# A four-layer graph network on one core: bias and edge-mean products taken out of the layer products, and edge lists of 214 instead of 216 rows per partition

## The reference, cut to what matters

```python
h = relu(layernorm(x))
# layer 0: attention over all edges in both directions, 4 heads, then two dense products
out = segment_sum(gr[dst] * alpha, src)
x = x + gelu(concat([out, h]) @ W1.T + b1) @ W2.T + b2
# layer 1: two rounds; nbr_r, the mean of the edge attributes at dst, is the same in both
nbr_r = segment_sum(edge_attr, dst) * inv_deg
nbr_x = segment_sum(h[src], dst) * inv_deg
h = relu(concat([h, nbr_x, nbr_r]) @ W + b)
# layer 2: one round of the same kind, without the edge attributes
y = concat([h[tgt], h[src] - h[tgt]]) @ W + b, then the mean over the edges of a node
# layer 3: attention with 8 heads, layer norm, a feed-forward product with biases, layer norm
```

## Time and profile before

| what | value |
|---|---|
| median of 3 runs | 5928.51 us (5918.02 to 5931.22) |
| profiled execution, own time | 5926.62 us |
| its span | 5923.7 us |
| busy share DVE, POOL, PE, ACT | 68%, 60%, 45%, 21% |
| mean granted TensorE clock | 0.607 of full speed |

### The profile page before, as it was taken

One profiled execution on the slowest core, in us unless ns is written; L12 is line 12 of the kernel. 1 busy time (PEld: TensorE's weight loads), 2 busy tenths in 40 slices (PEclk: granted clock), 3 DMA queues, 4 the chain that ended last, 5 costly groups with the idle time before them and its releaser, 6 DMA issues.

```text
span 5923.7 us, 53534 instructions
## 1 busy us (share of the span) xinstructions
PE 2662.1 (45%) x13332; PEld 1808.8 (31%) x13333; DVE 4000.1 (68%) x6981; ACT 1264.8 (21%) x4424; POOL 3582.9 (60%) x3760
## 2 busy tenths in 40 slices
PE   1795101011211323333333542776762777777646
PEld 1570101001211323323322442554641323323215
DVE  9778888888875777877877882223232676767655
ACT  0000000000000111111111110000001777777731
POOL 2777777777777777777777743000005777777730
PEclk6555555555555555555555555767765888888876
DMA  6222121212222333333333320635431223323230
GB/s 234 58 58 50 49 55 49 76 41 51 51 65 55 84 78 85 77 80 83 78 81 80 86 70 22 215 105 172 135 99 23 73 82 82 84 80 89 73 101 6
DMA packets 391629, 476.62 MB, mean 80 GB/s; under 512 B 215693, under 2 KB 251599, under 8 KB 384256
## 3 DMA queue, kind: packets, MB, share of 16 engines
q1 hardware_dynamic: 135840, 279.78, 14.4%
q0 software_dynamic: 114832, 133.36, 11.0%
q10 hardware_dynamic: 140752, 61.28, 3.7%
HBM read 294.88 MB, written 179.24 MB: 80 GB/s over the span
## 4 chain that ended last, share of the span: by engine, by line
POOL 50%; issue 20%; DVE 13%; PE 11%; DMA 5%; ACT 0%; POOLq 0%; DVEq 0%; SPq 0%; ACTq 0%
POOL arena L779 35%; POOL rec_dram L736 11%; PE acc L2039 4%; DMA oh<-mt_dram 2%; DVE OHX L1473 2%; PE acc L1854 2%; PE acc L1856 1%; PE acc L2023 1%; POOL own_dram L756 1%; DMA V<-in_edge_attr_dram 1%; DMA rec_dram<-V,rowst 1%; PE acc L1990 1%; DVE oh L1483 1%; DVE arena L1495 1%; DVE V L1515 1%
## 5 line engine op out<-in xcount | busy, mean ns | idle before, releaser
L779 POOL DMA_INDIRECT arena<-tab_dram,jst x2592 | 2519.3, 972 | 778.1 <-issue 775.0
L736 POOL DMA_INDIRECT rec_dram<-V,rowst x784 | 837.5, 1068 | 231.6 <-issue 224.0
L729 POOL TENSOR_TENSOR pdum<-pdum 128x1 f32<-128x1 f32 x197 | 53.1, 270 | 1122.5 <-DVE arena L1681 869.3
L1982 PE MATMUL pw<-OHX 128*128 128x128 bf16 x1632 | 209.3, 308 | 789.3 <-DVE OHX L1473 788.7
L1990 PE MATMUL acc<-arena,oh 128*128 128x64 f32 x1952 | 423.1, 417 | 252.0 <-DVE oh L1483 252.0
L1990 PEld LDWEIGHTS acc<-arena,oh 128*128 128x128 f32 x1952 | 413.3, 327 | 266.3 <-issue 266.3
L946 ACT ACTIVATE arena<-arena,ew 128x64 f32<-128x64 f32 x1728 | 417.8, 333 | 33.4 <-PE acc L2063 33.4
L2063 PE MATMUL acc<-OHX,ident 128*128 128x512 f32 x432 | 253.8, 753 | 370.6 <-ACT OHX L946 370.6
L946 ACT ACTIVATE OHX<-arena,ew 128x64 f32<-128x64 f32 x1728 | 417.8, 333 | 2.5
L1982 PEld LDWEIGHTS pw<-OHX 128*128 128x128 bf16 x1632 | 155.8, 140 | 840.5 <-DVE OHX L1473 840.5
L1495 DVE TENSOR_TENSOR arena<-arena,pt 128x1024 f32<-128x1024 f32 x108 | 131.8, 1221 | 383.3 <-DMA arena<-tab_dram,jst 381.2
(11 more groups left out here) (535 smaller groups left out, 6281.4 us busy)
## 6 DMA issues: line engine op xcount, KB each, us to landing
oh<-mt_dram SPq DMA_DIRECT2D x90, 512.0 KB, 3.6
arena<-tab_dram,jst POOLq DMA_INDIRECT x2592, 2.5
arena<-rec_dram SPq DMA_DIRECT2D x122, 288.0 KB, 3.6
mt_dram<-oh ACTq DMA_DIRECT2D x272, 128.0 KB, 1.8
oh<-mt_dram SPq DMA_DIRECT2D x75, 416.0 KB, 3.9
oh<-mt_dram SPq DMA_DIRECT2D x75, 384.0 KB, 3.9
rows_dram<-V SPq DMA_DIRECT2D x27, 1056.0 KB, 4.0
rows_dram<-arena SPq DMA_DIRECT2D x27, 1056.0 KB, 4.3
```

Source lines behind the costliest of these rows:

```text
L736: gp.indirect_dma_start(rec[:, :], bass.IndirectOffsetOnAxis(ap=rowst[:, q, k:k + 1], axis=0), recst[:, q, k, :], None).then_inc(S[f"scat{ ...
L779: gp.indirect_dma_start(hd.G[:, a.r, j, :], None, table[:, :], row_of(jst[:, a.r, j:j + 1])).then_inc(S[f"{x}g{a.r}"], 16)
L1982: last = nc.tensor.matmul(unit_bank(c.slot)[:, k // 2 * P:(k // 2 + 1) * P], mones[c.slot][:, 0, k, :], mones[c.slot][:, 1, k, :], start=k ...
```

## The change

1. RU = 214 rows per partition are used; the layout in DRAM keeps its 216. In the last block of each list the last two rows are empty, so 24 gathers are issued there instead of 32 (blocks 26 and 53 of layer 0, block 26 of layer 3), and DVE waits for as many (`gathered`). POOL's loop over the blocks of layer 0 is cut in two, with blocks 24 to 27 written out between.
2. The transposes of nbr_r and its products with both rounds' W1b are made once, while POOL runs the 50 gathers at the end of layer 0. DVE adds the bias to each and keeps the results in NBW (SBUF). The transposes use tile pw. In the same wait DVE adds the bias of layer 0's second product to X.
3. No product has a bias matmul any more. DVE adds NBW or the broadcast bias to the product after it (rounds 0 to 2); in the last feed-forward product DVE adds the bias to Hn while PE works.
4. The copy of Hn into CAT moves from the end of each round to its start.
5. `bias` is a tile of 128 partitions, filled by broadcasting DMAs at the start. `row_index` and the list stage have one small DVE instruction more for each call.

```diff
--- before.py
+++ after.py
 RP, RB, RK = 216, 8, 4
+RU = 214
 RH = RB // 2
 TB = RB * RK
 NBL = RP // RB
 NB0, NB3 = 2 * NBL, NBL
-ROWS = P * RP
...
+        NBW = [OHXf[:, k * NC * D:(k + 1) * NC * D].rearrange("p (c d) -> p c d", d=D) for k in (2, 3)]
...
+        def short(a):
+
+            return isinstance(a.g, int) and a.g % NBL == NBL - 1
+
+        def gathered(a):
+
+            done = (a.turn + 1) * TB
+            if isinstance(a.g, int):
+                done -= sum(last <= a.g and last % 4 == a.r for last in range(NBL - 1, NB0, NBL)) * (RP - RU) * RK
+            return done * 16
...
-                sp.dma_start(bias[:, k, :], t[name].unsqueeze(0)).then_inc(S["wts"], 16)
+                sp.dma_start(bias[:, k, :], t[name].unsqueeze(0).to_broadcast([P, D])).then_inc(S["wts"], 16)
...
-                sp.dma_start(LB[:, l, :], lin[l][0:P * RP * RK].rearrange("(p x) -> p x", p=P)).then_inc(S["lbi"], 16)
+                sp.dma_start(LB[:, l, 0:RU * RK], lin[l][0:P * RU * RK].rearrange("(p x) -> p x", p=P)).then_inc(S["lbi"], 16)
...
                     hold(S[f"{x}j{a.r}"], (a.turn + 1) * 16, held[0] + a.g)
-                    for j in range(TB):
+                    for j in range(TB - (RP - RU) * RK if short(a) else TB):
                         gp.indirect_dma_start(hd.G[:, a.r, j, :], None, table[:, :], row_of(jst[:, a.r, j:j + 1])).then_inc(S[f"{x}g{a.r}"], 16)
                 if hd is heads0:
                     quads(gp, n, rows, 0, KEYS_AT // 4)
                     held[0] += KEYS_AT
                     gather_keys()
                     held[0] -= KEYS_AT
-                    quads(gp, n, rows, KEYS_AT // 4)
+                    quads(gp, n, rows, KEYS_AT // 4, NBL // 4)
+                    for t in range(4):
+                        rows(Group(NBL // 4, t))
+                    quads(gp, n, rows, NBL // 4 + 1)
                 else:
                     quads(gp, n, rows)
                 held[0] += n
...
-            exponentials("a", [CX0[1], CX0[2], FC0, FX0])
+            exponentials("a", [CX0[1], CX0[2], FC0])
+            transposed(D, NRT, pw)
+            exponentials("a", [FX0], 3)
             transposed(2 * D)
             ff_up(0, ACT.Gelu, D, b1c0)
             sqrt_()
             transposed(2 * D)
-            transposed(D, NRT)
             transposed(2 * D)
             sqrt_()
...
-                link(V.tensor_scalar(spare, nid, each, unused3, ALU.mult, ALU.add))
-                elsewhere(val[:, 0:NC], spare[:, 0:NC])
-                link(V.tensor_copy(dst[:, 2, :], spare[:, 0:NC]))
-                link(V.tensor_scalar(rowi, val, 1.0 / RP, None, ALU.mult))
...
+                link(V.scalar_tensor_tensor(rest, quo, float(RP - RU), val, ALU.mult, ALU.add))
+                link(V.tensor_scalar(spare, nid, each, unused3, ALU.mult, ALU.add))
+                elsewhere(rest[:, 0:NC], spare[:, 0:NC])
+                link(V.tensor_copy(dst[:, 2, :], spare[:, 0:NC]))
+                link(V.scalar_tensor_tensor(val, quo, float(2 * RP - RU), val, ALU.mult, ALU.add))
...
+                link(V.memset(lb[:, RU * RK:RP * RK], float(KEYEND)))
...
-                v.wait_ge(S[f"{x}g{a.r}"], (a.turn + 1) * 16 * TB)
+                v.wait_ge(S[f"{x}g{a.r}"], gathered(a))
...
+            def bias_of(k):
+
+                return bias[:, k, :].unsqueeze(1).to_broadcast([P, NC, D])
+            v.wait_ge(S["lin"], 3)
+            V.tensor_tensor(NBW[0], acc_n, bias_of(1), ALU.add).then_inc(S["act"], 1)
+            v.wait_ge(S["act"], 3)
+            link(V.tensor_tensor(X[:], X[:], bias_of(0), ALU.add))
+            v.wait_ge(S["lin"], 4)
+            link(V.tensor_tensor(NBW[1], acc_n, bias_of(2), ALU.add))
             v.wait_ge(S["aeg"], 2 * NC * 16)
             EM = E0[:, :, :, w0:]
...
+                link(V.tensor_copy(CAT[:, :, 0:D], Hn[:]))
...
-                link(V.tensor_copy(CAT[:, :, 0:D], Hn[:]))
                 link(V.tensor_reduce(XC, SUM3.rearrange("p (c k d) -> p c d k", k=3, d=D), AX, ALU.add))
                 link(V.tensor_tensor(CAT[:, :, D:2 * D], XC, deg_b, ALU.mult))
                 if r == 2:
                     link(V.tensor_tensor(CAT[:, :, D:2 * D], CAT[:, :, D:2 * D], Hn[:], ALU.subtract))
                 V.memset(vdum[:, 0:1], 0.0).then_inc(S["ev"], 1)
-                v.wait_ge(S["lin"], 4 + r)
+                v.wait_ge(S["lin"], 6 + r)
+                link(V.tensor_tensor(XC, acc_n, NBW[r] if r < 2 else bias_of(3), ALU.add))
                 if r == 0:
-                    link(V.tensor_scalar(Hn[:], acc_n, 0.0, None, ALU.max))
+                    link(V.tensor_scalar(Hn[:], XC, 0.0, None, ALU.max))
                     split_rows()
                     continue
                 if r == 1:
-                    link(V.tensor_scalar(XC, acc_n, 0.0, None, ALU.max))
+                    link(V.tensor_scalar(XC, XC, 0.0, None, ALU.max))
                 else:
-                    link(V.tensor_tensor(XC, acc_n, hasin[:].unsqueeze(2).to_broadcast([P, NC, D]), ALU.mult))
+                    link(V.tensor_tensor(XC, XC, hasin[:].unsqueeze(2).to_broadcast([P, NC, D]), ALU.mult))
                 link(V.tensor_tensor(X[:], X[:], XC, ALU.add))
...
-            v.wait_ge(S["lin"], 8)
-            link(V.tensor_tensor(Hn[:], Hn[:], acc_n, ALU.add))
+            link(V.tensor_tensor(XC, Hn[:], bias_of(4), ALU.add))
+            v.wait_ge(S["lin"], 10)
+            link(V.tensor_tensor(Hn[:], XC, acc_n, ALU.add))
...
-            def product(parts, width, bk=None):
+            def product(parts, width):
 
                 pe.wait_ge(S["tc"], ntp[0])
                 for c in range(NC):
                     o = acc[:, c * width:(c + 1) * width]
                     for n, (TL, K, R) in enumerate(parts):
-                        last = nc.tensor.matmul(o, TL[0:K, c * P:(c + 1) * P], R, start=n == 0, stop=n == len(parts) - 1 and bk is None)
-                    if bk is not None:
-                        last = nc.tensor.matmul(o, ones[0:1, :], bias[:, bk, :], start=False, stop=True)
+                        last = nc.tensor.matmul(o, TL[0:K, c * P:(c + 1) * P], R, start=n == 0, stop=n == len(parts) - 1)
                 last.then_inc(S["lin"], 1)
 
             def hidden(W, K, n0):
...
+            transposes(nbr_r[:], D, pw)
+            for k in range(2):
+                if k:
+                    pe.wait_ge(S["act"], 3)
+                product([(NRT, D, W1b[:, k, :])], D)
             pe.wait_ge(S["ev"], 3)
             transposes(CAT, 2 * D)
             hidden(WT[:, 2, :], 2 * D, 0)
-            product([(T2, D, WT[0:D, 3, :])], D, 0)
+            product([(T2, D, WT[0:D, 3, :])], D)
 
...
-                if r == 0:
-                    transposes(nbr_r[:], D)
-                if r < 2:
-                    product([(T, 2 * D, W1a[:, r, :]), (NRT, D, W1b[:, r, :])], D, 1 + r)
-                else:
-                    product([(T, 2 * D, WT[:, 4, :])], D, 3)
+                product([(T, 2 * D, W1a[:, r, :] if r < 2 else WT[:, 4, :])], D)
...
-            product([(T2, 2 * D, F2[:])], D, 4)
+            product([(T2, 2 * D, F2[:])], D)
```

More of the change, by code:

```diff
@@ L54 @@
 NB0, NB3 = 2 * NBL, NBL
-ROWS = P * RP
+ROWS = P * RU
 MW = 2 * TB + 3 * RB
@@ L307, in build @@
         attb = sb("attb", [P, D])
-        bias = sb("bias", [1, 5, D])
+        bias = sb("bias", [P, 5, D])
         lnb = sb("lnb", [P, 5, D])
@@ L693, in _ @@
                 sp.wait_ge(S[f"dwr{q}"], 16 * NB3)
[L694 removed]
+            sp.dma_start(TL3, rows3[0:P * RP, :].rearrange("(p f) w -> p f w", p=P)[:, RU - 1, :]).then_inc(S["dtl"], 16)
             sp.wait_ge(S["xp"], 1)
@@ L833, in _, with transposed @@
             ntc, nln = [0], [0]
-            def transposed(K, dst=None):
+            def transposed(K, dst=None, frm=pt):
                 for b in range(-(-NC // 4)):
@@ L839, in transposed @@
                     bank = (ntc[0] % 2) * 512
-                    A.copy((T if dst is None else dst)[0:K, b * 512:b * 512 + m], pt[0:K, bank:bank + m]).then_inc(S["tc"], 1)
+                    A.copy((T if dst is None else dst)[0:K, b * 512:b * 512 + m], frm[0:K, bank:bank + m]).then_inc(S["tc"], 1)
                     ntc[0] += 1
@@ L883, in _, with exponentials @@
                 act.wait_ge(S[f"scat{q}"], SG * 16 * GT)
-            def exponentials(x, bufs):
+            def exponentials(x, bufs, done=0):
                 for k, buf in enumerate(bufs):
-                    act.wait_ge(S[x + "cx"], k + 1)
+                    act.wait_ge(S[x + "cx"], done + k + 1)
                     A.activation(buf, buf, ACT.Exp).then_inc(S[x + "cb"], 1)
@@ L1150, in row_index @@
             def row_index(dst, val, unused0, unused3, each):
-                link(V.tensor_scalar(spare, nid, each, unused3, ALU.mult, ALU.add))
-                elsewhere(val[:, 0:NC], spare[:, 0:NC])
-                link(V.tensor_copy(dst[:, 2, :], spare[:, 0:NC]))
```

(27 more changed lines are left out.)

3 lines of the change are left out of this document (1 added, 2 removed).

## The result

The changed kernel takes 5765.2 us (median of 4 runs, 5761.9 to 5767.3), the kernel before 5926.8 us beside it: a ratio of 0.9729 [0.9712, 0.9745]. The forecast was 5774 us, between 5757 and 5795 us. The profiled execution took 5767.3 us with a span of 5765.6 us, 158.1 us less span than before. Beside the first eight experiments the kernel before itself took 7911 us (chip 11) and 7916 us (chip 0), so that from those runs only short stretches of the trace can be used; beside the last four it took 5926.0 us (chip 2) and 5927.4 us (again a chip with the number 0).

A forecast was written before the change was run, and what follows sets the result against it. POOL's gathers pace the attention; in rounds and feed-forward parts DVE waits for PE's products. Products -134.3, X add +1.0, fewer gathers -9.9 and -9.9: -153.1 us from 5926.6, said as 5774 us, range 5757 to 5795.

The forecast's parts named there:

- What stays of the waits: DVE's five product waits keep 13.7 us (layer 0), 6.2 us in each round and 16.1 us (last).
- The products at 9.8, 9.8, 9.8, 9.8 and 10.9 us: Five products without bias matmuls take 50.1 us together instead of 184.4; 134.3 us saved, bounds 106.9 to 152.9.
- alternation: In products, taking turns between 128- or 64-row stationary tiles and the one-row tile costs extra: 0.31 us per instruction.
- rival B: The shorter products run at the fast clock from end to end: 18.6 us more saved, 5755 us; chance 0.07.
- The moved work at 0: Transposes, two products and adds, some 33 us, hide in layer 0's wait for 50 gathers, done over 30 us early.
- The X add at +1.0 us (0 to 1.8): DVE's add of the bias to X, both inputs in SBUF, holds POOL's gathers at layer 0's end: +1.0 us.
- Biases on DVE, copies moved, net 0: In the rounds three adds of about 1.85 us come, three copies of 1.82 us become hidden; +5.5 us without cover.
- Block 26 of layer 0, -9.9: Eight fewer gathers put POOL 9.9 us ahead, and all of it arrives at block 48: -9.9 us.
- block 53, 0: Layer 0's last block: DVE comes without a wait, so eight fewer gathers are worth 0, at most 9.9 us.
- Block 26 of layer 3, -9.9: Eight fewer gathers ahead of a DVE that waits 10.20 us in the last block: -9.9 us.
- Rival D: New lists make each of 2568 gathers dearer; 0.060 us each eats the gain, 0.07 gives 5953 us; chance 0.02.

The follow-up runs named there:

- bias_matmul_b: Changed kernel with one-row bias matmuls back behind each of the 25 matmuls of the three round products and the last product: 5856.3 us, ratio 0.9875.
- copy_at_end: Changed kernel with the copy of Hn into CAT back behind the neighbour sums of each round: 5767.5 us, ratio 0.9732.
- products_only_b: Changed kernel with lists of 216 rows per partition and all 2592 gathers again, run on another chip: 5780.5 us, ratio 0.9757.
- block26_full_b: Changed kernel with 32 gathers again in block 26 of layer 0 only: 5774.5 us, ratio 0.9743.
- extra_128: Changed kernel with one more 128-row accumulating matmul behind each of 25 in four products: waits 60.7 us (rounds), 32.2 us (last product).
- products_only: Changed kernel with lists of 216 rows per partition and all 2592 gathers again: 7753 us beside 7911 us, ratio 0.982.

## Why the prediction was right, step by step

**What stays of the waits**: right. The waits are 20.6 us for layer 0, 38.5 for the rounds and 27.3 for the last product with the covered add (forecast 23.5, 3 x 16 and 27), 86.4 us together. Without their products, 38.9 us, they keep 47.5 us, where the forecast kept 48.4 (13.7 + 3 x 6.2 + 16.1).

**The products at 9.8, 9.8, 9.8, 9.8 and 10.9 us**: the mechanism, alternation, was right and is shown; the size was 11.2 us off (50.1 forecast, 38.9 measured). The term that was mis-sized is the clock. I took it that four products begin fast and slow down on the way, as the one at 33.25 us does. In rounds 1 and 2 the granted clock was 1.00 until the product ended; in layer 0 and round 0 it fell on the way (0.54 from 3640.00 to 3644.30 us in layer 0's). The windows of the changed kernel over the product of round 1 and the second half of round 0's (engines' busy us and instructions, PEclk, DMA share, GB/s):

```profile
4083.00:4089.00 6.00, 5.79 (x50) 5.66 (x50) 0.08 (x1) 0.04 (x1) 0.00 (x0) 1.00 0.00 0
3871.00:3875.50 4.50, 4.48 (x21) 4.29 (x21) 0.00 (x0) 0.00 (x0) 0.00 (x0) 0.50 0.00 0
```

So rival B was right for two of the five products, and 146.4 us lies between the forecast 134.3 and its bound of 152.9.
The rule of the Trainium skill behind B (TensorE: Matmul & The Clock Gate, "What's actually happening": the throttled clock is the default and activity releases it) fits rounds 1 and 2. It does not fit round 0, nor this window of bias_matmul_b, in which PE is never idle and stays at 0.50:

```profile
4364.00:4390.00 26.00, 26.00 (x86) 21.02 (x85) 0.00 (x0) 0.00 (x0) 0.00 (x0) 0.50 0.00 1
```

**The moved work at 0**: right. The second moved product ended at 3563.4, the last add at 3565.4, and the gathers landed at 3611.0; 45.7 us were left, more than the 30 forecast; the first product, for one, took 6.87 us where 10.9 was taken for it.

**The X add at +1.0 us (0 to 1.8)**: it holds POOL, by less. DVE's line 1630 and the gather beside it:

```profile
3552.49 1.86 DVE L1630 TENSOR_TENSOR X<-X,bias 128x1600 f32<-128x1600 f32 x1
```

```profile
3552.50 0.95 POOL L825 DMA_INDIRECT arena<-rows_dram,rend_u  x1 [0.30 <-issue]
3553.75 1.42 POOL L825 DMA_INDIRECT arena<-rows_dram,rend_u  x1 [0.30 <-issue]
```

1.42 - 0.94 = 0.5 us. The gather that began with the add was not touched; only the next, which began 0.6 us ahead of the add's end, became longer. By the rule of the Trainium skill (SBUF — State Buffer, "SBUF: two separate sides") the port would be taken for the whole 1.86 us. That is more than the 0.5 us measured here.

**Biases on DVE, copies moved, net 0**: right. The adds take 1.82 us each behind the products, and copy_at_end shows 2.0 us for each copy in the line.

**Block 26 of layer 0, -9.9; block 53, 0**: right, by the holds (10.3 and 0.4 us). Block 48 begins at 3279.31 us where it began at 3289.80.

**Block 26 of layer 3, -9.9**: the place is right, the sum is not. DVE waits 0.45 us there instead of 10.20, and the last block took 11.7 us less. The row of the changed kernel:

```profile
5520.56 0.42 DVE L1765 TENSOR_TENSOR sc<-arena 128x256 f32<-128x256 f32 x1 [0.45 <-DMA arena<-tab_dram,jst]
```

But the layer gave 2.8 us. The step that failed is the one that read the stage as fixed up to its last block. The first 26 blocks took this long (from the stage's second hold, at 4384.64 us in the changed kernel, to the one ahead of the last block):

| kernel | lists | us |
|---|---|---|
| before | 216 | 1093.2 |
| products_only_b | 216 | 1094.4 |
| changed kernel | 214 | 1100.3 |
| block26_full_b | 214 | 1101.2 |
| bias_matmul_b | 214 | 1099.9 |
| copy_at_end | 214 | 1093.5 |

I first took it that the shorter lists made the blocks slower, which products_only_b bore out. copy_at_end has the short lists and the fast blocks: that theory fell. What differs from block to block is where DVE's fourth multiply (line 1717 before, 1748 after) falls among the gathers. A slow block of before (42.1 us), DVE and POOL, and a fast one (41.2 us):

```profile
5309.00 2.48 DVE L1717 TENSOR_TENSOR arena<-arena,ew 128x1024 f32<-128x1024 f32 x2 [2.58 <-PE acc L2063]
```

```profile
5309.19 1.85 POOL L779 DMA_INDIRECT arena<-tab_dram,jst  x1 [0.30 <-issue]
```

```profile
5391.61 0.94 POOL L779 DMA_INDIRECT arena<-tab_dram,jst  x1 [0.30 <-issue]
5392.86 0.98 POOL L779 DMA_INDIRECT arena<-tab_dram,jst  x1 [0.30 <-issue]
```

In the first the gather that begins 0.2 us behind the multiply is held by 0.9 us. In the second the multiply began at 5391.79, 0.2 us behind a gather, and cost POOL next to nothing (0.98 us). Of four blocks of before in a row one is such a fast one (41.2 us); in the changed kernel none is, from the eighth block on: they go about 42.5, 42.2 and 41.6 us in turn. Over 26 blocks this is 7 us. What puts a kernel into the one or the other pattern stays open: when the stage starts does not sort the rows of the table, nor do the lists. Each row is one execution, so the pattern may as well change from one execution of a kernel to the next; no run here tells. Rival D priced dearer gathers at 0.060 us each for the new lists; what is seen is 7.0 / 832 = 0.008 us in this stage, and it does not go with the lists.

The errors went against each other: 12.1 us more from the waits for products (11.2 of it the products, 0.9 what stays), 7.1 us less from layer 3, 0.5 us more from layer 0, 1.0 us forecast for the X add and 1.5 us of small losses measured. 12.1 - 7.1 + 0.5 + 1.0 - 1.5 = 5.0 us is the distance from the forecast 153.1 to the 158.1 of the spans. That the total fell so near its forecast is in part luck, all the more as the clock of the products differs from one execution to the next.

## What to carry to other kernels

With f32 matmuls of 64 columns, look at whether the stationary tile keeps its row count. 25 one-row bias matmuls behind the 25 of a product cost 16 to 23 us here, more than the product itself (5.8 to 10.9 us); one broadcast add on VectorE costs 1.8 us. If such matmuls must stay, issue them in a row of their own (7 to 13 us here). Where POOL issues gathers beside DVE's two-input instructions, the time of a stage can hang on how the two fall on each other, 7 us in 1100 here, and none of these edits steered it. Keep some us of range for such a stage, and judge an edit there by holds on both sides of it, not by the whole time.

## What the runs showed that I had not expected

The clock of equal products is not repeatable from round to round: of the three rounds the changed kernel was slowed in round 0, copy_at_end in round 1 (8.52 us against 5.79), and products_only_b and block26_full_b in none. In round 2 of extra_128 100 instructions ran at the granted clock 1.00 from end to end, in 11.4 us.

Beside the first eight experiments the kernel before took 7911 and 7916 us, as said. The time is lost where POOL issues indirect DMAs, and most of all in the first stage. The window from 500 to 750 us (busy us and instructions of each engine, PEclk, DMA share, GB/s) of the kernel before, and of products_only there:

```profile
500.00:750.00 250.00, 69.15 (x155) 25.81 (x153) 208.25 (x401) 6.55 (x44) 197.51 (x197) 0.50 0.19 49
```

```profile
500.00:750.00 250.00, 18.29 (x101) 10.24 (x100) 6.38 (x12) 6.55 (x44) 175.91 (x202) 0.50 0.18 49
```

POOL issues as much as before, ACT does its 44 instructions, but DVE does 12 in place of 401. In the attention of layer 0 DVE and POOL both go on, only slower: DVE has 411 instructions from 3000 to 3500 us in products_only, and 524 in the kernel before. In the rounds, where POOL is idle, the waits are nearly the same (39.2 us against 38.5 us). The cause was not looked for. It need not be the chip: chips recorded under the number 0 stand on both sides. By whole time an effect of 20 us could not be told there.
